# Four-layer block: bf16 terms of the projections formed on TensorE and read from PSUM, mask rows of two buffers placed by DMA

## The reference, cut to what matters

```python
# layer 0: 16 heads of 8
Q = jnp.einsum('bsd,hdk->hbsk', q, W_query)
K = jnp.einsum('bsd,hdk->hbsk', q, W_key)
V = jnp.einsum('bsd,hdv->hbsv', q, W_val)
attn = jax.nn.softmax(norm * jnp.einsum('hbqk,hbnk->hbqn', Q, K), axis=-1)
# layer 3: 16 heads of 8, a local window of 32 beside a latent attention
Q, K, V = x @ wq, x @ wk, x @ wv        # split into heads
local = _local_window_attn(Q, K, V)     # softmax over the allowed keys of two blocks of 32
gl = jax.nn.sigmoid(jnp.einsum('bhsd,hd->bhs', Q, gate_local_w))
```

## Time and profile before

| what | us |
|---|---|
| median of 3 runs | 1849.66 |
| the profiled execution, its own time | 1848.59 |
| its span, first to last instruction | 1846.7 |
| mean granted clock of TensorE, share of full | 0.791 |
| DVE, PE, ACT, POOL busy | 1327.5, 1201.1, 827.3, 244.5 |
| projection stage of layer 0, PE's start to SP's next DMA | 20.9 to 41.46 |
| projection stage of layer 3, PE's start to PE's start of the next stage | 1376.87 to 1398.71 |

### The profile page before, as it was taken

How to read it: one execution, slowest core, us unless ns; L and a number is a source line. 1 busy time by engine, 2 the same in 40 slices (tenths; PEclk the granted TensorE clock), 3 DMA queues, 4 the chain that set the end, 5 groups by cost and what they waited for, 6 DMA issues and landing times. The chain is left out here.

```text
span 1846.7 us, 28995 instructions
## 1 busy us (share of the span) xinstructions
PE 1201.1 (65%) x10365; PEld 589.1 (32%) x10366; DVE 1327.5 (72%) x3500; ACT 827.3 (45%) x1541; POOL 244.5 (13%) x258
## 2 busy tenths in 40 slices
PE   4799999999999995659843630503157898221053
PEld 2122222222222233449733410201134566210043
DVE  5999999999999905473473359596977785767701
ACT  4089999999999993122210230300023455100021
POOL 4000000000000000114103140300032210000123
PEclk9589999999999997679965865756567989555577
DMA  2101000100010000000034310000014020200012
GB/s 57 45 6 30 22 19 22 29 24 19 20 29 26 2 2 15 28 1 2 1 117 144 86 43 0 1 1 0 0 37 137 23 52 4 95 0 1 5 47 63
DMA packets 44889, 57.95 MB, mean 31 GB/s; under 512 B 11990, under 2 KB 35609, under 8 KB 44346
## 3 DMA queue, kind: packets, MB, share of 16 engines
q1 hardware_dynamic: 39769, 50.40, 9.2%
q0 software_dynamic: 3712, 4.96, 1.1%
q10 hardware_dynamic: 1264, 0.72, 0.2%
HBM read 29.22 MB, written 13.63 MB: 23 GB/s over the span
## 5 line engine op out<-in xcount | busy, mean ns | idle before, releaser
L724 ACT ACTIVATE l0att_probs<-l0att_ps_sv 128x512 f32<-128x512 f32 x1024 | 555.7, 596 | 84.4 <-PE l0att_ps_sv L694 72.3
L761 DVE TENSOR_REDUCE l0att_half_negmax<-l0att_ps_m 128x1 f32<-128x1024 f32 x480 | 547.0, 1213 | 6.4 <-PE l0att_ps_m L633 6.4
L663 PE MATMUL l0att_ps_sv<-l0att_probs,l_V_aug 128*32 128x256 f32 x4096 | 331.2, 392 | 5.3 <-ACT l0att_pv_sb L715 5.3
L694 PE MATMUL l0att_ps_sv<-l_Q,l_K 51*128 51x512 bf16 x1024 | 201.0, 389 | 2.5 <-ACT l0att_probs L724 0.2
L633 PE MATMUL l0att_ps_m<-l_K,l_Q 48*128 48x512 bf16 x960 | 186.2, 385 | 11.0 <-DVE l0att_half_negmax L761 7.1
L663 PEld LDWEIGHTS l0att_ps_sv<-l0att_probs,l_V_aug 128*32 128x32 f32 x4096 | 83.2, 108 | 199.6 <-issue 105.0
L694 PEld LDWEIGHTS l0att_ps_sv<-l_Q,l_K 51*128 51x128 bf16 x1024 | 49.5, 92 | 216.7 <-ACT l0att_probs L724 204.1
L350 PE MATMUL ada_ps<-ident_sb,xn 128*128 128x128 f32 x112 | 31.2, 442 | 87.5 <-DVE xn L338 87.0
L2740 PE MATMUL l3sel_ps_c<-l3sel_part,l3sel_ones 128*128 128x15 bf16 x56 | 10.9, 195 | 99.0 <-DVE l3sel_part L2765 99.0
L2929 ACT ACTIVATE l3mlp_rowsT<-l3mlp_ps_t,l3f_norm_l_lncols 128x512 f32<-128x512 f32 x4 | 3.1, 777 | 160.7 <-PE l3mlp_ps_t L2897 160.5
L413 POOL CAST l0att_nm<-l0att_negmax 128x16 bf16<-128x16 f32 x16 | 3.1, 197 | 514.1 <-DVE l0att_negmax L737 514.1
(11 more groups left out here) (584 smaller groups left out, 2262.0 us busy)
## 6 DMA issues: line engine op xcount, KB each, us to landing
l_Q<-l_qp SPq DMA_DIRECT2D x188, 32.0 KB
l_K<-l_kp SPq DMA_DIRECT2D x188, 32.0 KB
l1ffn_W<-in_l_expert_w_dram SPq DMA_DIRECT2D x1, 4096.0 KB
l3f_mlp_l_w<-in_l_w_dram SPq DMA_DIRECT2D x2, 2048.0 KB
l_sorted_in<-l1ffn_zeros SPq DMA_DIRECT2D x1, 3072.0 KB
l1exp_rows<-l_sorted_in SPq DMA_DIRECT2D x6, 512.0 KB, 7.4
l_sorted_out<-l1exp_y SPq DMA_DIRECT2D x6, 512.0 KB, 4.6
l_Q<-l_q_parts SPq DMA_DIRECT2D x18, 128.0 KB
```

What stands on the lines that cost most here:

```text
L663: mm = pe.matmul(ps_v[32 * c:32 * c + 32, cols], V_aug[:, kt, h, :], probs[:, kt % 2, c, cols], start=(kt == 0 and part == 0), stop=(kt == ...
L694: pe.matmul(ps_s[:, (n + i) % 3, :], K[at, h % HEAD_BUFS, c1(kt)], Q[at, h % HEAD_BUFS, c4(2 * pair + i)], start=True, stop=True).then_inc ...
L724: act.activation(probs[:, kt % 2, c, :], ps_s[:, n % 3, :], ACT.Exp).then_inc(expd, 1)
L761: dve.tensor_reduce(half_negmax[:, h % 2, t, half:half + 1], src, AX_X, ALU.max, negate=True).then_inc(m_read, 1)
```

## The change

In `stage_project_parts` k comes first and q second, in eight chunks of one bank each. For each chunk PE makes the fp32 product; ACT reads it as bf16, which is the high term; PE adds the high term times the negative identity into the same bank (`minus16`, a new constant of 32 KB, loaded by `Loads`), which leaves the remainder in PSUM; DVE reads it as bf16, the middle term; PE subtracts that too; and the low term is read from the bank, by DVE for even chunks and by ACT for odd ones. PE's queue is written out in steps: the product of chunk s, the first subtraction of chunk s-2, the second of chunk s-4, and from step 8 on the values' matmuls of one bank. ACT's copies of the values come behind all its reads of terms, one per bank. The scale of q goes into the weights first. The fp32 `q` is kept only in the fourth layer, by an extra read of ACT; `k`, the remainders and POOL's part are gone. SP stores each term of k, then of q, once its four chunks are read.

The mask rows of buffers 0 and 1 are loaded by DMA for all four heads, with the heads' dimension of the source repeated, two transfers for each buffer. DVE copies no mask rows. ACT's copies for buffer 2 read all four heads' rows from buffer 0.

The diff, cut: the removed body of `stage_project_parts` stands in the listing above.

```diff
@@ -421,82 +421,101 @@
-def stage_project_parts(nc, loads, w_name, g, name, V_aug, q, qp, kp, drams=(), stored=None, first=None):
+def stage_project_parts(nc, loads, w_name, g, name, V_aug, qp, kp, q=None, drams=(), stored=None):
+    CHUNKS = 2 * NC4
...
+        minus = loads["minus16"]
+        ps = st.ps("ps", [P, CHUNKS, BANK])
...
+        def term(n, i):
+            return (kp, qp)[n // NC4][i][:, c4(n % NC4)]
...
             @block.sync
             def _(sp):
+                for m, (parts, dram) in enumerate(zip((kp, qp), drams)):
+                    read = NC4 * (m + 1)
+                    sp.wait_ge(high_read, read)
+                    sp.dma_start(dram[0], parts[0][:]).then_inc(stored, 16)
+                    sp.wait_ge(middle_read, read)
+                    sp.dma_start(dram[1], parts[1][:]).then_inc(stored, 16)
+                    for done in low_read:
+                        sp.wait_ge(done, read // 2)
+                    sp.dma_start(dram[2], parts[2][:]).then_inc(stored, 16)
 
             @block.tensor
             def _(pe):
                 pe.wait_ge(loads.done, loads.all)
+                for s in range(CHUNKS + 4):
+                    if s < CHUNKS:
+                        if s == NC4:
+                            pe.wait_ge(scaled, 1)
+                        pe.matmul(ps[:, s, :], w[:, 1 - s // NC4, :], g.hT[:, c4(s % NC4)], start=True, stop=True,
+                                  skip_group_check=True).then_inc(full_done, 1)
+                    if 2 <= s < CHUNKS + 2:
+                        n = s - 2
+                        pe.wait_ge(high_read, n + 1)
+                        pe.matmul(ps[:, n, :], minus[:], term(n, 0), start=False, stop=True,
+                                  skip_group_check=True).then_inc(rest_done, 1)
+                    if s >= 4:
+                        n = s - 4
+                        pe.wait_ge(middle_read, n + 1)
+                        pe.matmul(ps[:, n, :], minus[:], term(n, 1), start=False, stop=True,
+                                  skip_group_check=True).then_inc(last_done, 1)
+                    if s >= CHUNKS:
+                        j = s - CHUNKS
+                        pe.wait_ge(low_read[j % 2], j // 2 + 1)
+                        for t in range(4 * j, 4 * j + 4):
+                            mm = pe.matmul(ps[:, j, c1(t % 4)], g.hT[:, c1(t)], w[:, 2, :], start=True, stop=True)
                         mm.then_inc(v_done, 1)
 
             @block.scalar
             def _(act):
+                act.wait_ge(loads.done, loads.all)
+                act.activation(w[:, 0, :], w[:, 0, :], ACT.Identity, scale=L0_K ** -0.5).then_inc(scaled, 1)
+                for s in range(CHUNKS + 4):
+                    if s < CHUNKS:
+                        act.wait_ge(full_done, s + 1)
+                        if q is not None and s >= NC4:
+                            act.activation(q[:, c4(s - NC4)], ps[:, s, :], ACT.Identity)
+                        act.activation(term(s, 0), ps[:, s, :], ACT.Identity).then_inc(high_read, 1)
+                    n = s - 4
+                    if n >= 0 and n % 2 == 1:
+                        act.wait_ge(last_done, n + 1)
+                        act.activation(term(n, 2), ps[:, n, :], ACT.Identity).then_inc(low_read[1], 1)
                 for j in range(NC4):
                     act.wait_ge(v_done, j + 1)
-                    for t in range(4):
-                        act.activation(V_aug[:, 4 * j + t, :, 0:L0_K],
-                                       ps[:, j, c1(t)].rearrange("p (h k) -> p h k", h=L0_H), ACT.Identity)
+                    act.activation(V_aug[:, 4 * j:4 * j + 4, :, 0:L0_K],
+                                   ps[:, j, :].rearrange("p (t h k) -> p t h k", t=4, h=L0_H), ACT.Identity)
 
             @block.vector
             def _(dve):
+                for s in range(CHUNKS + 2):
+                    if s < CHUNKS:
+                        dve.wait_ge(rest_done, s + 1)
+                        dve.tensor_copy(term(s, 1), ps[:, s, :]).then_inc(middle_read, 1)
+                    n = s - 2
+                    if n >= 0 and n % 2 == 0:
+                        dve.wait_ge(last_done, n + 1)
+                        dve.tensor_copy(term(n, 2), ps[:, n, :]).then_inc(low_read[0], 1)
...
-                pool.wait_ge(chunk_read, 2 * NC4)
-                rest_parts(Chain(pool, pool_chain), pool, [p[:, POOL_COLS] for p in kp], pool_rest[:], k[:, POOL_COLS],
-                           pool_parts_done)
-                pool.wait_ge(pool_parts_done, 1)
...
@@ -819,7 +838,7 @@
...
-        for_parts = Loads(nc, d, st, "parts", "l0_wqkv")
+        for_parts = Loads(nc, d, st, "parts", "l0_wqkv", "minus16")
@@ -833,9 +852,7 @@
...
-        with Stage(nc, "l0q") as st_q:
-            q = st_q.sb("q", [P, S])
-            stage_project_parts(nc, for_parts, "l0_wqkv", g, "l0proj", V_aug, q, qp, kp)
+        stage_project_parts(nc, for_parts, "l0_wqkv", g, "l0proj", V_aug, qp, kp)
@@ -2170,18 +2187,11 @@
...
-def load_mask_rows(sp, d, Q, K, placed):
+def load_mask_rows(sp, d, Q, K, buf, placed):
...
-        sp.dma_start(operand[0][0:MASK_ROWS, 0, :], d[name]).then_inc(placed, 16)
-
-
-def copy_mask_rows(copy, operand, buf, copied):
-
-    heads = slice(1 if buf == 0 else 0, GROUP)
-    n = heads.stop - heads.start
-    copy(operand[buf][0:MASK_ROWS, heads, :],
-         bcast(operand[0][0:MASK_ROWS, 0:1, :], MASK_ROWS, n, S + WINDOW)).then_inc(copied, 1)
+        sp.dma_start(operand[buf][0:MASK_ROWS],
+                     bcast(d[name].unsqueeze(1), MASK_ROWS, GROUP, S + WINDOW)).then_inc(placed, 16)
@@ -2359,8 +2369,6 @@
...
-                for operand in (Q, K):
-                    copy_mask_rows(dve.tensor_copy, operand, 1, mask_copied)
@@ -2483,7 +2492,10 @@
...
-                            pe.wait_ge(mask_copied[grp % GROUP_BUFS], 2)
+                            if grp % GROUP_BUFS < 2:
+                                pe.wait_ge(mask_placed[grp % GROUP_BUFS], 16 * 2)
+                            else:
+                                pe.wait_ge(mask_copied, 2)
@@ -2544,8 +2556,10 @@
...
+                act.wait_ge(mask_placed[0], 16 * 2)
...
-                    copy_mask_rows(lambda out, in_: act.activation(out, in_, ACT.Identity), operand, 2, mask_copied[2])
+                    act.activation(operand[2][0:MASK_ROWS], operand[0][0:MASK_ROWS], ACT.Identity)\
+                       .then_inc(mask_copied, 1)
@@ -2625,17 +2639,16 @@
...
-        for_parts = Loads(nc, d, st, "parts", "l3_wqkv")
+        for_parts = Loads(nc, d, st, "parts", "l3_wqkv", "minus16")
...
-        mask_placed = st.sem("mask_placed")
-        mask_copied = [st.sem(f"mask_copied{b}") for b in range(GROUP_BUFS)]
-        load_mask_rows(nc.sync, d, Q, K, mask_placed)
+        mask_placed = [st.sem(f"mask_placed{b}") for b in range(2)]
...
+            load_mask_rows(nc.sync, d, Q, K, b, mask_placed[b])
@@ -2648,19 +2661,13 @@
...
-            def first_masks(dve):
-                dve.wait_ge(mask_placed, 16 * 2)
-                for operand in (Q, K):
-                    copy_mask_rows(dve.tensor_copy, operand, 0, mask_copied[0])
-
-            stage_project_parts(nc, for_parts, "l3_wqkv", g, "l3proj", V_aug, q, qp, kp,
-                                (q_parts, k_parts), stored, first_masks)
-            stage_l3_latent(nc, for_latent, g, q, rem, gates, Q, K, q_parts, k_parts, stored, loaded, mask_copied[1])
+            stage_project_parts(nc, for_parts, "l3_wqkv", g, "l3proj", V_aug, qp, kp, q, (k_parts, q_parts), stored)
+            stage_l3_latent(nc, for_latent, g, q, rem, gates, Q, K, q_parts, k_parts, stored, loaded)
...
-            stage_l3_local(nc, d, for_local, g, V_aug, Q, K, q_parts, k_parts, loaded, constants_placed, mask_copied, O)
+            stage_l3_local(nc, d, for_local, g, V_aug, Q, K, q_parts, k_parts, loaded, constants_placed, mask_placed, O)
@@ -3012,7 +3019,7 @@
...
-BF16_CONSTANTS = ("ident16", "lat_causal", "local_mask_q", "local_mask_k", "before", "not_yet",
+BF16_CONSTANTS = ("ident16", "minus16", "lat_causal", "local_mask_q", "local_mask_k", "before", "not_yet",
@@ -3031,7 +3038,7 @@
...
-        "ident16": bits16(np.eye(P)),
+        "ident16": bits16(np.eye(P)), "minus16": bits16(-np.eye(P)),
...
```

## The result

The changed kernel took 1856.11 us, the median of 16 runs (1849.74 to 1862.73), against 1851.24 us for the kernel before on the same chip (16 runs). The ratio is 1.0026, with a 95% interval of 1.0015 to 1.0038: 4.8 us slower (2.8 to 7.0). The prediction was 1850.2, range 1843.5 to 1857.0. The time lies in the range, but by another route than the one I had forecast.

What follows compares the result with a forecast made beforehand. DVE was busiest (72% of the span), with its maxima untouched, so only two short stages and their surroundings could change. Terms -1.2 + 6.1 - 2.0 - 1.3 = +1.6 on 1848.59 gave 1850.2 us, range 1843.5 to 1857.0.

Steps and rivals of the forecast that it cites:

- rival D: Norm stage: mask data at 221 GB/s or less, SP released at 1387, 4.6 us longer than forecast; 1854.8 us; chance 0.15.
- The first attention: First attention's projection: the new pipeline of terms ends at 39.9 against 40.90; 1.0 us gained, 1.2 kept in the sum.
- switch cost of 1.0 us: Projection on PE: an fp32 matmul behind a bf16 one starts 0.31 us later, not 0.21, some ten times; between 0 and 2.
- SP held in the norm stage: Fourth layer's norm stage: SP, issuing four mask transfers, ends at 1382.5 and the projection starts late; 6.1 us lost.
- a bound of 1.6 MB on the way: SP's queue: SP runs three transfers, 1.6 MB, ahead, then goes at the data's pace until 3.2 MB have moved, 10 us.
- The estimate of 303 GB/s: Mask transfers: 72 rows would run on 12 engines, turning an estimate from 404 GB/s into 303 GB/s and 10.6 us.
- The projection's body: Fourth layer's projection: 19.35 us from start to end against 21.3, with 5 us until the clock rises; 2.0 us gained.
- The clock in the latent stage: Latent stage: after only 2.3 us of idle PE the full clock may stay; 1.3 us gained, between 0 and 3.0.
- What would show it: Signs: SP's end near 1378.4 or past 1381, projection's start minus ACT's end, pass distances, PE's end, values' reads, L2253's duration.
- A: Norm stage: no stall of SP, 2.0 us lost instead of 6.1; 1846.1 us; chance 0.22.
- C: As A, and the clock stays up at the latent stage (3.0) and switches cost little; 1842.7 us; chance 0.13.
- E: Projections: each step waits for ACT or DVE, 0.3 us per subtraction, or values' reads add 1.0; to +8, 1856; chance 0.08.

Runs made afterwards that it cites:

- e6_rows_64_and_8: The changed kernel with each mask transfer cut into one of 64 rows and one of 8 rows: 1862.92 us, one run.
- e1: The changed kernel with all four mask transfers issued in the latent stage, behind the loads of the first two groups: 1844.27 us, ratio 0.9970.
- e7: The changed kernel with each mask transfer cut by columns into two, pieces of 2080 B: 1855.47 us, one run.
- e10: The changed kernel with all four mask transfers ahead of all six of constant rows, still in the norm stage: 1877.99 us, one run.
- e4: The kernel before with the new projections in both attentions and the mask copies as before: 1847.85 us, ratio 0.9978.
- e9: The changed kernel with only the second buffer's masks moved to the latent stage, behind the loads of the groups: 1855.04 us, ratio 1.0026.
- e11: The changed kernel with each mask transfer cut by columns into pieces of 4096 B and of 64 B: 1861.00 us, one run.
- e8: The kernel of e1 with the reads of the values' matmuls spread, two earlier on ACT and one on DVE: 1841.94 us, ratio 0.9950.
- e12: The kernel of e9 with the reads of the values' matmuls spread as in e8: 1851.73 us, ratio 1.0001.
- e5_wide_rows: The changed kernel with mask rows stored four times in DRAM, so each transfer has 72 pieces of 16,640 B: 1854.04 us, one run.

## Why the prediction was right, point by point

The number held (1850.2 in a range to 1857.0, measured 1856.11) because two sizes were wrong in opposite senses. That is luck: the largest term was out by more than a factor of two, and the time lies 0.9 us under the upper end of the range, which had been drawn to take in rival D and the lower part of E. The sum of the terms was +1.6 us. The traces give -2.4 (the first attention, by its own experiment) + 13.4 - 4.0 - 2.7 = +4.3, and the measurement +4.8.

**The first attention**, forecast -1.2: -3.0 in its own stage, -2.4 in the end. The mechanism was right and PE's work too large. The switch cost of 1.0 us is nothing: 0.21 and 0.22 us between starts where an fp32 pass follows a bf16 one at full clock., from which I had taken it, shows another pair of shapes. PE ends 15.6 us after its start, not 17.15, and ACT 1.7 later (1.85 forecast; the strided writes of the values cost nothing, 2.06 us for four reads).

**SP held in the norm stage**, forecast +6.1: +13.4. This is the step that failed, in three ways. The mechanism, a bound of 1.6 MB on the way read from the earlier trace rows, is not there: four transfers of 1.2 MB go out in 1.9 us. What the runs show in its place is a long wait at the issue directly behind the transfer of 64 B pieces that is queued behind the masks; in the kernel before the same order was harmless, as 0.6 MB were ahead. Why that place, stays open. The rate, taken between 221 and 404 GB/s (3.2 MB in 10 us are 320), was 174. The stores are a bad model for these loads, and so was even the lower row; the old masks' own 144 pieces, which moved at 167, were in the same trace and not counted. And an issue of a mask that is not held takes 0.40 to 0.50 us with four pieces for each row, not 0.70, which made the least loss of 2.0 us too large. From 1372.5 to SP's release it took 15.8 us; even my outer bound was 14.5. Rival D had the outcome and the place: 1387 for SP's release (1388.3), 1854.8 for the time.

The DMA share speaks for one half of what I had cited. Seventy-two rows ran at a DMA share of 0.79, near 12 of 16, and 64 and 8 rows at 1.05. By the Trainium skill (DMA: Bandwidth & Descriptors, "Why a DMA increments its semaphore by 16 and not by 1") this is what the divisor of the slowest dimension gives, and the trace agrees. The records of the small pieces fit it too. In the changed kernel L2200 issues 192 pieces of 64 B, behind two masks of 72 rows, at 1371.83. A quarter of that number, 48, moved at 1375 while the masks went on, as they would if four engines were free of masks, and the next only after 1384. With masks of 64 rows (e6_rows_64_and_8, issue at 1375.14) none moved before 1384.7. The estimate of 303 GB/s built on it was wrong, since the rate was not set by the number of engines: more of them brought 178.

**The projection's body**, forecast -2.0: -4.0, for the same reason as in the first attention, and with the clock up within 4 us of the start (0.55 in 1389 to 1393, 1.00 in 1393 to 1397), not 5.

**The clock in the latent stage**, forecast -1.3 between 0 and 3.0: -2.7 in this trace, and in others 1.0 (6.3 against 5.3). I had chosen the middle, and it is in truth one or the other. Of the eight traces with 2.05 us of idle PE there, four kept the clock and four lost it. In the four that kept it (the changed kernel, e1, e7, e10) it had risen 2.9 to 4.6 us behind the start of the projection, in the four that lost it (e4, e6, e9, e11) 4.9 to 6.1 us behind it. That is a pattern of eight traces, and no run tests it.

**What would show it**: an end of SP past 1381, the start of the projection minus ACT's end as the price, L2253's duration: these were the right places. Not foreseen: that SP's first store would be held as well (harmless).

**Rivals.** A and C fall in the changed kernel by the 8.07 and 4.78 us. C comes true once the masks stand elsewhere: 1844.27 against its 1842.7. E falls: PE has no hole inside the projection. Its price was too low besides: 0.3 us for 32 subtractions are 9.6 us, so its upper end, with the values' reads, was above 1860 and not 1856.

## What to carry to other kernels

A transfer can cost the engine that issues it more than its issue when the queue is long (here 8 and 15 us for 0.4), and the one that pays is whoever stands behind it, here the barrier at a stage's end. Before large transfers are put on a queue, count what the same transfers moved in the trace of before (here 167 GB/s), and look where that engine has slack (here the latent stage, with over 40 us until the first reader) and what small transfers follow them: the same 4.8 MB cost 13 us ahead of the norm stage and nothing there. When a work-saving change frees an engine, place the new transfers as carefully as the old work was placed.

## What the runs showed of the hardware

- The issue directly behind a transfer of 204 pieces of 64 B waited 7.95 to 8.42 us with 2.4 MB queued ahead (five kernels), 15.49 us with 4.8 MB, 0.51 us with 0.6 MB. Without such a transfer in between, four transfers of 1.2 MB were issued in 0.40, 0.42, 0.42 and 0.50 us; the first constant transfer behind them waited 3.10 us.
- In stretches of four us the masks' loads ran at 154 to 182 GB/s in the changed kernel (pieces of 4160 B, DMA share 0.78 to 0.81), at 189 to 191 with 2080 B, at 160 to 164 when cut into 4096 and 64 B, and at 155 to 202, 178 in the mean, when cut into 64 and 8 rows (share 1.04 to 1.08): a third more of the engines' time brought 4% by these stretches, 9% by the time in which the first two masks' pieces began.
- Pieces of 64 B that were issued behind two transfers of 72 rows (the changed kernel): 48 moved some 3 us behind their issue, at 1374.9 to 1375.2, while the large transfers went on, and the next some 10 us later. Behind transfers of 64 and 8 rows the first moved 9.6 us behind the issue.
- With PE idle for 2.05 us before the latent stage, its eight passes took 3.62 us in four traces (the changed kernel, e1, e7, e10) and 5.30 to 5.32 us in four (e4, e6, e9, e11): the clock was kept in some executions and fell to 1.2 GHz in others. With 0.98 us of idle time it was kept both times (e8, e12), 3.62 us, and so it was once with 3.88 us (e5_wide_rows).
